# One LoRA tile fewer for slot 0 of block 1 in an attention and LoRA-MoE kernel

## The reference, cut to what matters

```python
# x: (4096, 512) after attention and layer norm; E=8 experts, R=32, F=1792
probs = softmax(x @ Wg.T); rw, sel = top_k(probs, 2); rw = rw / rw.sum(-1)
base1, base3 = x @ W1.T, x @ W3.T
for k in range(2):                       # two slots
    e = sel[:, k]
    x1 = base1 + (A1[e] @ x) @ B1[e]     # LoRA of the slot's expert
    x3 = base3 + (A3[e] @ x) @ B3[e]
    x2 = silu(x1) * x3
    out += (x2 @ W2.T + (A2[e] @ x2) @ B2[e]) * rw[:, k]
```

## Time and profile before

| what | value |
|---|---|
| median of 3 runs | 1919.02 us (1916.45 to 1919.62) |
| profiled execution | 1918.05 us, span 1916.2 us |
| TensorE matmuls busy | 1820.9 us, 95%, 8121 instructions |
| VectorE busy | 1081.6 us, 56%, 2119 instructions |
| ScalarE busy | 681.3 us, 36% |
| block 1 | 517.07 to 768.55 us |
| mean granted TensorE clock | 0.971 |

### The profile page before, as it was taken

One profiled execution on the slowest core, in us unless ns is written; L12 is line 12 of the kernel. 1 busy time (PEld: TensorE's weight loads), 2 busy tenths in 40 slices (PEclk: granted clock), 3 DMA queues, 4 the chain that ended last, 5 costly groups with the idle time before them and its releaser, 6 DMA issues.

```text
span 1916.2 us, 23371 instructions
## 1 busy us (share of the span) xinstructions
PE 1820.9 (95%) x8121; PEld 1473.0 (77%) x8121; DVE 1081.6 (56%) x2119; ACT 681.3 (36%) x1258; POOL 159.7 (8%) x208
## 2 busy tenths in 40 slices
PE   7885799999899999999999999999999999999996
PEld 5543577888688887888888888888888888888885
DVE  3677355555554446555655565556555555555554
ACT  4552433333232222343334333332343234323331
POOL 0025200000100000100010001000100110010000
PEclk9886799999999999999999999999999999999998
DMA  6313576555455442675377537753775377536651
GB/s 215 132 70 103 160 228 212 188 182 182 145 166 177 154 148 84 232 269 191 130 244 257 193 131 246 258 195 129 247 254 193 136 241 258 194 134 220 211 174 55
DMA packets 186572, 351.42 MB, mean 183 GB/s; under 512 B 52764, under 2 KB 93216, under 8 KB 182872
## 3 DMA queue, kind: packets, MB, share of 16 engines
q1 hardware_dynamic: 173984, 324.85, 50.1%
q0 software_dynamic: 11840, 24.91, 3.8%
q10 hardware_dynamic: 632, 0.16, 0.1%
HBM read 294.55 MB, written 55.28 MB: 183 GB/s over the span
## 4 chain that ended last, share of the span: by engine, by line
PE 90%; DVE 5%; DMA 1%; issue 1%; ACT 1%; POOL 1%; ACTq 0%; DVEq 0%; POOLq 0%
PE dp L635 32%; PE xB L635 26%; PE xA L635 25%; PE dp L806 1%; PE dp L659 1%; PE xA L683 1%; PE xB L683 1%; PE fb L835 1%; DMA mask<-hot_scr 0%; PE fb L711 0%; ACT xs_f L1027 0%; PE xA L649 0%; PE dp L743 0%; DMA wg_nat<-in_L_ffn_Wg 0%; DMA hot_scr<-hot_t 0%
## 5 line engine op out<-in xcount | busy, mean ns | idle before, releaser
L635 PE MATMUL xA<-xt_hi,upb 128*128 128x512 f32 x896 | 295.7, 391 | 0.0
L635 PE MATMUL xB<-xt_hi,upb 128*128 128x512 f32 x896 | 295.6, 391 | 0.0
L1582 DVE TENSOR_TENSOR gate<-gate,rw 128x512 f32<-128x512 f32 x112 | 77.6, 692 | 353.8 <-ACT gate L1195 353.8
L635 PE MATMUL dp<-dnb,s_hi 128*128 128x512 f32 x896 | 275.8, 389 | 0.0
L1551 DVE TENSOR_TENSOR acc<-dp,acc 128x512 f32<-128x512 f32 x224 | 154.9, 691 | 164.5 <-PE dp L635 164.5
L635 PEld LDWEIGHTS dp<-dnb,s_hi 128*128 128x128 f32 x896 | 168.3, 188 | 35.0
L635 PE MATMUL xB<-am_hi,upl 128*128 128x512 f32 x560 | 195.2, 397 | 0.0
L635 PEld LDWEIGHTS xA<-xt_hi,upb 128*128 128x128 f32 x896 | 168.2, 188 | 34.8
L635 PEld LDWEIGHTS xB<-xt_hi,upb 128*128 128x128 f32 x896 | 168.2, 188 | 34.6
L635 PE MATMUL xA<-am_hi,upl 128*128 128x512 f32 x560 | 192.3, 392 | 0.0
L635 PE MATMUL dp<-dnb,s_lo 128*128 128x512 f32 x448 | 174.3, 389 | 0.0
(11 more groups left out here) (284 smaller groups left out, 2907.6 us busy)
## 6 DMA issues: line engine op xcount, KB each, us to landing
upb<-upb_scr SPq DMA_DIRECT2D x196, 512.0 KB, 4.6
upl<-upl_scr SPq DMA_DIRECT2D x196, 256.0 KB, 2.9
dnb<-dnb_scr SPq DMA_DIRECT2D x98, 512.0 KB, 3.5
dnl<-dnl_scr SPq DMA_DIRECT2D x196, 128.0 KB, 4.0
upb_scr<-upb SPq DMA_DIRECT2D x14, 1024.0 KB, 5.4
A_sel<-a_scr SPq DMA_DIRECT2D x12, 1024.0 KB, 6.5
row<-in_x SPq DMA_DIRECT2D x32, 256.0 KB, 8.5
x_scr<-row SPq DMA_DIRECT2D x8, 1024.0 KB, 4.3
```

What stands on the lines that cost most here:

```text
L635: mm = pe.matmul(dst, lhs, rhs, start=start and x == 0 and y == 0, stop=x == len(operands) - 1 and y == 2, skip_group_check=True)
L1582: v.tensor_tensor(gate0[j][:, :], gate0[j][:, :], rw[:, 0, :], ALU.mult).then_inc(gate, 1)
```

## The change

Block 1 (`SEMI = 1`) takes 512 left-over tokens all of whose slot 0 experts lie in one half. The plan swaps the places of blocks 0 and 1 in the left-over tokens if needed (`swap`), and writes the number of the tile for slot 0 into `tsemi`. `parts(b)` lists the pairs of slot and tile of a block; for block 1 it is (0, 2), (1, 0), (1, 1), where tile 2 is a third tile in SBUF (`upl_semi`, `dnl_semi`), loaded from DRAM by the register's number. Slot 1 of block 1 still uses both tiles; block 0 is as before. The numbers of the dp banks, of the loads and of the masking units follow from the list.

In SBUF, the new tiles lie where `up_nat` was. `masked` masks slot 0's product with both masks and adds the two (through `s_raw`), so that slot 0 has one unit for each half of the A products instead of two.

```diff
+SEMI = 1
+def parts(b):
+    if b == SEMI:
+        return [(0, 2), (1, 0), (1, 1)]
+    return [(s, t) for s in range(2) for t in range(2)] if b < MIXED else [(0, 0), (1, 1)]
+
+def loads_at(b, n):
+    return sum(PAIRS * len({t for _, t in parts(x)}) for x in range(1, b)) + n * len({t for _, t in parts(b)})
 def pair_tiles(b):
-    return 2 * tiles(b) + TT
+    return len(parts(b)) + TT
 def masked_units(b):
+    if b == SEMI:
+        return [(2 * m + t, m, s, t) for m in range(2) for t, s in ((0, 1), (1, 0), (1, 1))]
...
+        natural.close()
+        upl_semi, dnl_semi = pair("upl_semi", [P, 2, 2, P], f32r), pair("dnl_semi", [P, 2, P], f32r)
+        def up_tile(j, t):
+            return upl_semi[j][:, :, :, :] if t == 2 else upl[j][:, t, :, :, :]
+        def dn_tile(j, t):
+            return dnl_semi[j][:, :, :] if t == 2 else dnl[j][:, t, :, :]
...
             def tile_of(b, s):
-                if b < MIXED:
+                if b == SEMI and s < 2:
                     return s
+                if b == SEMI and s not in chosen:
+                    sp.wait_ge(idx_done, 2)
+                    chosen[s] = sp.value_load(tsemi[0:1, 0:1], min_val=0, max_val=1)
+                if b == SEMI:
+                    return chosen[s]
                 if (b, s) not in chosen:
-                    sp.wait_ge(idx_done, 3)
+                    sp.wait_ge(idx_done, 4)
...
-                for s in range(2):
-                    sp.dma_start(flat(upl[j][:, s, :, :, :]).rearrange("p m s c -> p (m s c)"),
+                for s in sorted({t for _, t in parts(b)}):
+                    sp.dma_start(flat(up_tile(j, s)).rearrange("p m s c -> p (m s c)"),
                                  upl_scr[c, tile_of(b, s), :, :]).then_inc(upl_in[j], 16)
...
-                        pool.wait_ge(idx_done, 2)
+                        pool.wait_ge(idx_done, 3)
...
             def lora(b, j, m, s):
-                if b < MIXED:
-                    return [(upl[j][:, t, m, 0, :], upl[j][:, t, m, 1, :], am_hi[:, m, s, t, :], am_lo[:, m, s, t, :])
-                            for t in range(2)]
-                return [(upl[j][:, s, m, 0, :], upl[j][:, s, m, 1, :], am_hi[:, m, s, 0, :], am_lo[:, m, s, 0, :])]
+                many = sum(x == s for x, _ in parts(b)) > 1
+                return [(up_tile(j, t)[:, m, 0, :], up_tile(j, t)[:, m, 1, :], am_hi[:, m, s, t if many else 0, :],
+                         am_lo[:, m, s, t if many else 0, :]) for x, t in parts(b) if x == s]
...
             def down_g(b, g):
                 k = dp_pair(b, g)
-                for s, (hi, lo) in enumerate(((p_hi, p_lo), (q_hi, q_lo))):
-                    for t in range(tiles(b)):
-                        x = t if b < MIXED else s
-                        dst = dp_tile(k)
-                        product(dst[:, :], [(dnl[j][:, x, 0, :], dnl[j][:, x, 1, :], hi[j][:, :], lo[j][:, :])
-                                            for j in range(2)], True).then_inc(dp_ready, 1)
-                        k += 1
+                for s, t in parts(b):
+                    hi, lo = (q_hi, q_lo) if s else (p_hi, p_lo)
+                    dst = dp_tile(k)
+                    product(dst[:, :], [(dn_tile(j, t)[:, 0, :], dn_tile(j, t)[:, 1, :], hi[j][:, :], lo[j][:, :])
+                                        for j in range(2)], True).then_inc(dp_ready, 1)
+                    k += 1
...
-                link(v.tensor_scalar(mx[:, :], at_mixed[:, :], bnd[:, 0:1], dlt[:, 1:2], ALU.is_ge, ALU.mult))
+                link(v.tensor_scalar(swap[:, :], bnd[:, 1:2], float(S), float(S), ALU.is_ge, ALU.mult))
+                v.tensor_scalar(at_left[:, 0:TT], at_mixed[:, 0:TT], swap[:, 0:1], None, ALU.add)
+                link(v.tensor_scalar(at_left[:, TT:2 * TT], at_mixed[:, TT:2 * TT], swap[:, 0:1], None, ALU.subtract))
+                link(v.tensor_scalar(mx[:, :], at_left[:, :], bnd[:, 0:1], dlt[:, 1:2], ALU.is_ge, ALU.mult))
...
                 v.tensor_copy(idx[:, 0:MIXED * TT], mx[:, :]).then_inc(idx_done, 1)
+                v.tensor_scalar(tsemi[:, :], swap[:, :], 0.0, None, ALU.is_equal).then_inc(idx_done, 1)
...
-                    v.tensor_tensor(xn[n % 2][:, :], dp[dp_bank(dp_a(b, t))][:, :], mask[b % 2][:, s, x, :], ALU.mult)\
-                     .then_inc(am_raw, 1)
+                    if b == SEMI and x == 0:
+                        v.tensor_tensor(s_raw[:, :], src[:, :], mask[b % 2][:, 0, 0, :], ALU.mult)
+                    if b == SEMI and s == 0:
+                        link(v.tensor_tensor(xn[n % 2][:, :], src[:, :], mask[b % 2][:, 0, 1, :], ALU.mult))
+                        v.tensor_tensor(xn[n % 2][:, :], xn[n % 2][:, :], s_raw[:, :], ALU.add).then_inc(am_raw, 1)
+                    else:
+                        v.tensor_tensor(xn[n % 2][:, :], src[:, :], mask[b % 2][:, s, x, :], ALU.mult)\
+                         .then_inc(am_raw, 1)
```

More of the change, by code:

```diff
@@ L68, in dp_o @@
 def dp_o(b, g, i):
-    return dp_pair(b, g) + 2 * tiles(b) + i
+    return dp_pair(b, g) + len(parts(b)) + i
 def dp_a(b, t):
@@ L167, with last_of_tile, lows_at @@
     UNIT_AT.append(UNIT_AT[-1] + len(masked_units(_b)))
+def last_of_tile(units, n):
+    return n + 1 == len(units) or units[n + 1][0] != units[n][0]
+def lows_at(b, n):
+    return sum(not last_of_tile(masked_units(x), i) for x in range(b + 1)
+               for i in range(n + 1 if x == b else len(masked_units(x))))
 def build(nc, io, out):
@@ L197, in build @@
         upb, upl = [sb("upb0", [P, 2, 2, H], f32r)], [sb("upl0", [P, 2, 2, 2, P], f32r)]
-        up_nat, dn_nat = sb("up_nat", [P, UPB + LORA]), sb("dn_nat", [P, DNB + ER])
         acc, tab = [sb("acc0", [P, TT, H])], pair("tab", [P, TT, TABLE])
@@ L202, in build @@
         idx, ids = sb("idx", [P, B * TT], u32), [sb(f"ids{j}", [P, TT], u32) for j in range(2)]
-        tsel = sb("tsel", [P, 2, PURE], i32)
+        tsel, tsemi = sb("tsel", [P, 2, PURE], i32), sb("tsemi", [P, 1], i32)
+        natural = ExitStack()
+        dn_nat = sb("dn_nat", [P, DNB + ER])
+        up_nat = sb("up_nat", [P, UPB + LORA], at=natural)
         with ExitStack() as early:
@@ L255, in build @@
             mx, mx2 = fr("mx", [P, MIXED * TT]), fr("mx2", [P, MIXED * TT])
+            swap, at_left = fr("swap", [P, 1]), fr("at_left", [P, MIXED * TT])
             px = fr("px", [P, PURE, TT])
+        natural.close()
[4 more added lines that the diff above has]
+            return dnl_semi[j][:, :, :] if t == 2 else dnl[j][:, t, :, :]
         upb.append(sb("upb1", [P, 2, 2, H], f32r))
@@ L425, in load_dn @@
                       .then_inc(dn_in[j], 16)
-                    for s in range(2):
-                        sp.dma_start(flat(dnl[j][:, s, :, :]).rearrange("p s c -> p (s c)"),
+                    for s in sorted({t for _, t in parts(b)}):
+                        sp.dma_start(flat(dn_tile(j, s)).rearrange("p s c -> p (s c)"),
                                      dnl_scr[2 * g + j, tile_of(b, s), :, :]).then_inc(dn_in[j], 16)
@@ L875, in down_inputs @@
                     if b:
-                        pe.wait_ge(dn_in[j], 48 * ((b - 1) * PAIRS + g + 1))
+                        pe.wait_ge(dn_in[j], 16 * ((b - 1) * PAIRS + g + 1 + loads_at(b, g + 1)))
                     else:
@@ L948, in chunk @@
                 if b:
-                    pe.wait_ge(upl_in[j], 32 * loads)
+                    pe.wait_ge(upl_in[j], 16 * loads_at(b, c // 2 + 1))
                 pe.wait_ge(seed1, n + 1)
@@ L1144, in masked_hi @@
                     act.wait_ge(am_raw, UNIT_AT[b] + n + 1)
-                    act.activation(am_hi[:, m, s, x, :], xn[n % 2][:, :], ACT.Copy).then_inc(amh, 1)
+                    act.activation(am_hi[:, m, s, 0 if b == SEMI and s == 0 else x, :], xn[n % 2][:, :], ACT.Copy)\
+                       .then_inc(amh, 1)
             def highs(b, c):
@@ L1403, in plan @@
                 link(v.tensor_tensor(dlt[:, 2:3], dlt[:, 2:3], cnt[:, 1:2], ALU.subtract))
-                link(v.tensor_scalar(mx[:, :], at_mixed[:, :], bnd[:, 0:1], dlt[:, 1:2], ALU.is_ge, ALU.mult))
-                link(v.tensor_scalar(mx2[:, :], at_mixed[:, :], bnd[:, 1:2], dlt[:, 2:3], ALU.is_ge, ALU.mult))
+                link(v.tensor_scalar(swap[:, :], bnd[:, 1:2], float(S), float(S), ALU.is_ge, ALU.mult))
+                v.tensor_scalar(at_left[:, 0:TT], at_mixed[:, 0:TT], swap[:, 0:1], None, ALU.add)
+                link(v.tensor_scalar(at_left[:, TT:2 * TT], at_mixed[:, TT:2 * TT], swap[:, 0:1], None, ALU.subtract))
+                link(v.tensor_scalar(mx[:, :], at_left[:, :], bnd[:, 0:1], dlt[:, 1:2], ALU.is_ge, ALU.mult))
+                link(v.tensor_scalar(mx2[:, :], at_left[:, :], bnd[:, 1:2], dlt[:, 2:3], ALU.is_ge, ALU.mult))
                 link(v.tensor_tensor(mx[:, :], mx[:, :], mx2[:, :], ALU.add))
-                link(v.scalar_tensor_tensor(mx[:, :], at_mixed[:, :], dlt[:, 0:1], mx[:, :], ALU.add, ALU.add))
```

(34 more changed lines are left out.)

## The result

The changed kernel takes 1907.92 us (median of 6 runs, 1906.49 to 1911.42) where the kernel before takes 1919.32 us (6 runs): a ratio of 0.9939, 95% interval 0.9924 to 0.9954. (The ratios here are those of the record, taken over the runs of both kernels; they can differ from the quotient of the two medians by one or two thousandths.) It is 11.4 us faster, not the 28 us that were forecast, and lies outside the range of 1886 to 1896.5. The profiled execution took 1908.94 us, its span 1907.2.

A forecast was written before the change was run, and what follows sets the result against it. The prediction took TensorE to bound the kernel, busy 1820.9 of 1916.2 us. Its terms, -28.56 (matmuls) + 0.65 (masking) + 0 (prologue) + 0 (transfers) = -27.91 us, gave 1890.6 us, range 1886 to 1896.5.

The forecast's parts named there:

- the sum, -28.56 + 0.65 + 0 + 0: Whole kernel: matmuls removed, masking added, prologue 0 and transfers 0 give -27.91 us.
- The prediction's own sign for it: Blocks 2 to 7: would stay of equal length if the forecast was right.
- The count of matmuls and their price: Block 1: 84 LoRA up-projection and 42 down-projection matmuls go, 126 x 0.2267 = 28.56 us.
- The six matmuls ahead of the last wait: End of block 1: the last pair's removed down matmuls count, 1.36 us, and TensorE's wait stays at 2.0 us.
- The masking: VectorE between blocks 0 and 1: block 1's A products finish masking later, +0.65 us, bounds 0 and +2.8.
- The prologue: Small VectorE instructions around the indices: at most some 1.1 us, hidden, so 0.
- Both covers: Prologue: the gather's wait for the scatter and VectorE's 1.74 us wait for the gathered table hide the added instructions.
- The transfers: Third-tile loads in block 1: some 5.5 MB more, covered by 14.96 us per load, cost 0.
- The clock: Rival, ends of blocks 0 and 1: a slow stretch goes or appears, 1889.0 or 1892.2 us; chance 0.22.
- Bare copies: Rival, block 1: shorter LoRA groups expose ScalarE's copies, 0.6 us per chunk, 8.4 us, 1899.0; chance 0.04.
- a late third tile: Rival, LoRA products' wait on upl_in, all 14 chunks: mild 1897.6 us, chance 0.03; slower, 1926 us, chance 0.02.
- the change doesn't do what it says: Rival, block 1: for instance slot 0 still multiplies with two tiles, 1919 us; chance 0.03.

The follow-up runs named there:

- The padded form: Changed kernel with tsemi 64 elements long instead of 1, against the kernel before: 1901.87 us against 1931.04, ratio 0.9858.
- 64 and 32 elements: Changed kernel with tsemi 64 or 32 elements long instead of 1: 1901.87 and 1917.43 us against 1931.04 for the kernel before, ratios 0.9858 and 0.9921.
- only the high part moved: Kernel before with an unused 4-byte tensor behind tsel, moving all behind it by 32 bytes: 1943.54 us against 1928.76, ratio 1.0077.
- both gaps: Kernel before with low tensors 32 bytes off a multiple of 64, upb1 and all behind it at multiples: 1945.72 us against 1928.76, ratio 1.0105.
- the sweep: Separate kernel of back-to-back matmuls alone on TensorE, operands moved by set bytes: 10.88 us for 48 at 0, 256 and 512, 11.00 to 11.38 between.

## Why the prediction was wrong

**The step that failed** is the sum, -28.56 + 0.65 + 0 + 0: it has no term for the matmuls that stay. The forecast took 0.2267 us per matmul from the earlier trace rows and let the other 7995 keep it, without a reason given; the only place that speaks of SBUF, the transfers' paragraph, says that the new tiles take the place of up_nat and leaves it at "no wait is added". For 2676 of the 7995 the price became 0.2333. At 0.08 / 12 us more each that is 17.8 us. The prediction's own sign for it was that blocks 2 to 7 keep their length, and that sign failed. Measured by stages, against a span that fell by 9.0 us:

- blocks 2 to 7: +12.35 us (1896 such matmuls, 12.6 by the count);
- block 1: 225.17 us instead of 222.9, +2.25 (252 base and LoRA products, 48 A products of block 2 and 24 closing ones: 2.2 by the count);
- between blocks 0 and 1: 38.53 us instead of 36.58, +1.95. From the first A product to the next down tile it is 18.29 us, before 16.43. The padded form has 17.10 there at the clock of the kernel before (0.90), so 0.67 is masking. The other 1.2 go with a lower clock in this execution (0.85) and with the dearer A products, which here end after VectorE's work: 14.01 us for 48. The closing products add 0.1;
- block 0's chunks: +0.64 us only, where the 348 matmuls with unmatched operands would give 2.3 by the count. There the chain goes over VectorE between TensorE's groups, and a group of 12 in the first even chunk took 2.75 to 2.79 us before and 2.79 to 2.82 after, so less is added to each; TensorE's busy time rose by 1.1 us.

The prologue ended 2.4 us later in the profiled execution (block 0's last A tile starts at 223.20 instead of 220.83). With block 1's 26.3 us less, this and the other stages make the 9.0 us. Of the 2.4, 2.26 us were there before the first instruction that the change adds (the cast to `pos_u`, 178.70 instead of 176.44). On one chip the same A tile starts at 232.58 and at 240.73 us in two kernels that differ in padding alone (64 and 32 elements), so I can't give the 2.4 to the change.

**What was right, by the steps:**

The count of matmuls and their price. The padded form takes 221.29 us for block 1; with the slow stretch of 1.6 us that the kernel before had at its end, and this execution has not, that is 222.9, as forecast. The six matmuls ahead of the last wait do count: the wait is still 2.0 us.

The masking. I put it at +0.65 us, from the second tile on. In the padded form the chain reads

```profile
504.14 0.70 DVE xn L1582
...
504.86 0.69 DVE xn L1583
...
506.26 0.69 DVE xn L1585
...
507.65 0.69 DVE s_raw L1580
...
509.65 0.70 DVE xn L1582
...
511.77 0.70 DVE xn L1585
...
512.50 0.64 ACT am_hi L1191
...
513.16 0.70 DVE am_lo L1567
...
513.91 3.04 PE dp L683 x12
```

From the second tile (504.14) to the last subtraction's end (513.86) it is 9.72 us, before 9.06 (491.69 to 500.75 in the earlier trace rows): +0.66. The units start at 504.14, 506.26, 507.65, 509.65 and 511.77: 2.12, 1.39, 2.00, 2.12 apart, where the forecast had 2.13, 1.39, 2.00, 2.13.

The prologue. The three small instructions cost 0.66 us on VectorE (indices 2.92 us later than before, where the cast to `pos_u` ahead of the plan is 2.26 later). Both covers hold in the sense that the gather still waits for the scatter and VectorE for the gathered table, as the timeline of the changed kernel shows; compare:

```profile
183.42 0.17 DVE L1459 CAST idx<-mx 128x8 uint32<-128x8 f32 x1
...
185.31 0.99 POOL L578 DMA_INDIRECT tab<-cls_scr,idx  x1 [1.43 <-DMA cls_scr<-tbl,pos_u]
...
192.71 0.17 DVE L1553 CAST ids<-tab 128x4 uint32<-128x4 f32 x1 [1.75 <-DMA tab<-cls_scr,idx]
```

From the cast to `pos_u` to the gather it is 6.61 us, before 6.64, so the indices cost it nothing. The copy of the gathered numbers came 2.90 us later, though, 0.64 more than the cast. From cast to copy the four kernels without the change have 13.29 to 14.31 us and the five with it 14.01 to 14.92, means 13.7 and 14.4: the ranges overlap, so a cost of some half a microsecond is neither shown nor ruled out.

The transfers. The whole execution moves 5.50 MB more (351.42 to 356.92), as counted; block 1 has 193 GB/s where it was 153, part of it because the block is shorter. No TensorE wait is for a DMA.

**The rivals.** The clock: in the execution of the kernel before, the wait at the end of block 0 was followed by no slow stretch and that of block 1 by one, 7.12 and 8.74 us for the 30 closing matmuls. The same kernel moved as a whole by 32 bytes had 7.09 and 7.12, the one with only the high part moved 8.77 and 8.79, both gaps 8.79 and 7.26. All four outcomes occur in kernels with the same instructions and other padding, so the instructions don't fix which wait is followed by a stretch at the lower clock; that one and the same kernel can show both was not seen (two executions of the changed kernel both had the stretch at the end of block 1 alone). That agrees with the Trainium skill's account (TensorE: Matmul & The Clock Gate, "What's actually happening") of an activity window that runs freely. It is worth 1.6 us each time, too little for the miss. Neither does the padded form owe its gain to it: its blocks 2 to 7 alone are 12.6 us shorter than the changed kernel's. Bare copies and a late third tile didn't occur: block 1's chain in the padded form has groups of 2.72 and 2.04 us without a gap. That the change doesn't do what it says is ruled out by the count. None of my rivals was the right one.

**What I could have seen.** The earlier trace rows gave one price for two buffers at different places, and the diff moved all that lies behind `tsel`. No row of the kernel before shows a dearer matmul, though, so I couldn't have priced it; I could only have named the edit and left room for it.

## What to carry to other kernels

When a diff adds or moves an allocation, even of 4 bytes, list which tensors shift against each other, and ask of the busiest engine's operands whether their distance changes; a small cost per instruction over the whole kernel can outweigh what the edit removes at one place. When the count of instructions fell as planned and the busy time didn't, compare stages that the change doesn't touch: if they grew with the same counts at the same clock, look for placement before contention. For streams of matmuls of this kind, keep stationary and moving operands a multiple of 256 bytes apart, by padding small tensors to a multiple of 256.

## What the runs showed of the hardware

With float32r operands, 128x128 stationary and 128x512 moving, at the full clock (1.00 in the sweep), each with its own weight load, matmuls start 0.2267 us apart if their operands' start addresses in the partition differ by a multiple of 256 bytes, and 0.229 to 0.237 us apart otherwise (0.229 at 64 bytes, 0.2333 at 32, 96, 128, 192 and 384, 0.237 at 4). The weight loads' own duration doesn't change (188 ns in both kernels); the latency of the matmuls goes from 389 ns to 396 (median on A_sel) or 395 (mean in the sweep at 32 bytes). Why the distance counts, no run here shows, and other operand types and shapes were not tried.
